# Two-layer graph network on one core: r is transposed by VectorE and DMA, W2 runs one graph later, ScalarE makes the second norm's statistics

## The reference

```
h = relu(layernorm(x))                          # per node, over 512
x = x + relu(attention(h, adj))                 # 8 heads of 64, masked softmax over neighbours
h = relu(layernorm(x))
r = relu(conv(h, adj, W1) + b1)                 # 512 -> 1024, conv mixes the nodes by adj
q = layernorm(r) * gamma + beta                 # over 1024
x = x + h + conv(q, adj, W2) + b2               # 1024 -> 512
```

## Time and profile before

| | us |
|---|---|
| median of 3 runs (2589.86 to 2593.36) | 2591.59 |
| the profiled execution | 2593.87 |
| its span, first to last instruction | 2591.9 |
| PE busy in the span | 2527.3 (98%) |
| DVE, POOL, ACT busy | 1968.6, 1630.6, 1423.3 |
| one turn in the middle | 19.52 |

### The profile page before, as it was taken

How to read it: one execution, slowest core, us unless ns; L and a number is a source line. 1 busy time by engine, 2 the same in 40 slices (tenths; PEclk the granted TensorE clock), 3 DMA queues, 4 the chain that set the end, 5 groups by cost and what they waited for, 6 DMA issues and landing times.

```text
span 2591.9 us, 50876 instructions
## 1 busy us (share of the span) xinstructions
PE 2527.3 (98%) x14996; PEld 2195.1 (85%) x14996; DVE 1968.6 (76%) x4640; ACT 1423.3 (55%) x3465; POOL 1630.6 (63%) x2068
## 2 busy tenths in 40 slices
PE   3899999999999999999999999999999999999998
PEld 2788888888888888888888888888888888888886
DVE  5877777777777777777777777777777777777774
ACT  2555555555555555555555555555555555555553
POOL 4666666666666666666666666666666666666663
PEclk8899999999999999999999999999999999999999
DMA  5122222222222222222222222222222222222210
GB/s 183 63 75 80 77 76 80 74 79 77 73 79 74 80 79 74 80 76 77 77 73 79 74 80 79 74 80 79 74 80 72 82 79 71 79 75 80 79 65 26
DMA packets 105480, 201.89 MB, mean 78 GB/s; under 512 B 20080, under 2 KB 36464, under 8 KB 105456
## 3 DMA queue, kind: packets, MB, share of 16 engines
q1 hardware_dynamic: 105456, 201.60, 23.5%
HBM read 167.39 MB, written 34.15 MB: 78 GB/s over the span
## 4 chain that ended last, share of the span: by engine, by line
PE 85%; DVE 8%; issue 3%; POOL 2%; DMA 1%; ACT 1%; SPq 0%; POOLq 0%; DVEq 0%
PE p_w1a L843 12%; PE p_w1a L839 12%; PE p_w1a L838 12%; PE p_att L917 7%; PE p_w1b L953 5%; PE p_w1b L839 5%; PE p_w1b L843 5%; PE p_w1b L838 5%; PE p_att L897 4%; PE p_fa L834 2%; PE p_fa L832 2%; PE p_fa L833 2%; PE p_fb L832 2%; PE p_fb L833 2%; PE p_fb L834 2%
## 5 line engine op out<-in xcount | busy, mean ns | idle before, releaser
L392 POOL TENSOR_TENSOR rs<-ve,halfpow 128x1 f32<-128x1 f32 x128 | 117.8, 921 | 544.8 <-DVE ve L774 544.8
L380 POOL TENSOR_TENSOR u<-u,mask 128x1024 f32<-128x1024 f32 x128 | 306.3, 2393 | 182.0 <-DMA u<-en_rows 182.0
L838 PE MATMUL p_w1a<-W_hi,rT_hi 128*128 128x512 f32 x1024 | 415.5, 406 | 0.0
L457 ACT ACTIVATE att<-u,shifts 128x128 f32<-128x128 f32 x1024 | 400.5, 391 | 18.4 <-DVE shifts L734 10.5
L839 PE MATMUL p_w1a<-W_lo,rT_hi 128*128 128x512 f32 x1024 | 404.1, 395 | 0.0
L458 ACT ACTIVATE att_low<-u,shifts 128x128 f32<-128x128 f32 x1024 | 399.5, 390 | 0.0
L843 PE MATMUL p_w1a<-W_hi,rT_lo 128*128 128x512 f32 x1024 | 280.8, 396 | 0.0
L502 ACT ACTIVATE rT_hi<-p_tb 128x512 fp32r<-128x512 f32 x128 | 76.6, 598 | 333.5 <-PE p_tb L864 333.5
L917 PE MATMUL p_att<-feats,attT 128*128 128x65 f32 x2048 | 242.9, 272 | 2.2 <-ACT attT L492 2.2
L917 PEld LDWEIGHTS p_att<-feats,attT 128*128 128x128 f32 x2048 | 239.6, 192 | 2.7 <-ACT attT L492 2.7
L789 DVE SCALAR_TENSOR_TENSOR raw<-p_w1a,rs,t_bc 128x512 f32<-128x512 f32 x128 | 96.1, 750 | 187.2 <-PE p_w1a L843 187.2
(11 more groups left out here) (125 smaller groups left out, 7216.9 us busy)
## 6 DMA issues: line engine op xcount, KB each, us to landing
u<-en_rows SPq DMA_DIRECT2D x130, 576.0 KB, 3.6
x_in<-in_x SPq DMA_DIRECT2D x128, 256.0 KB, 2.6
xT_in<-in_xT SPq DMA_DIRECT2D x128, 256.0 KB, 3.2
out<-raw SPq DMA_DIRECT2D x128, 256.0 KB, 2.0
adj_in<-in_adj SPq DMA_DIRECT2D x128, 128.0 KB, 2.5
en_rows<-eT SPq DMA_DIRECT2D x520, 1.1 KB
raw<-in_W1T SPq DMA_DIRECT2D x2, 1024.0 KB, 8.1
raw<-in_W2T SPq DMA_DIRECT2D x2, 1024.0 KB, 9.7
```

Of the source, the lines that this page charges most:

```text
L380: nc.gpsimd.tensor_tensor(u[:, g.slot(2), 0:HEADS, :], u[:, g.slot(2), 0:HEADS, :], mask[:, :].unsqueeze(1).broadcast_to([P, HEADS, N]), A ...
L392: nc.gpsimd.tensor_tensor(rs1[:, :], ve1[:, :], halfpow[:, :], ALU.pow).then_inc(s_rs1, 1)
L457: nc.scalar.activation(att[:, i, :], u[:, g.slot(2), i, :], ACT.Exp, bias=shifts[:, 0, i:i + 1])
L838: mm(dst, hi, w_hi, start=first, stop=False)
```

## The change

- **r is transposed without PE.** DVE transposes r, 128x1024, in blocks of 32x32 (STREAM_TRANSPOSE into rB); SP stores rB to a DRAM tensor r_blocks (512 KB), waits for it, and loads it back by four DMAs that put the blocks at their places (rT). Each of the four moves 1024 pieces of 32 elements (128 bytes).
- ACT rounds rT in one piece of 1024 at the end of the turn (rT_hi), DVE forms rT_lo in one piece at the start of the next turn, before the first pre. Both read rT in SBUF, where the two halves were read in PSUM.
- **W2, z and the product by G move back a graph**: in turn t PE multiplies graph t-1 by W2 and graph t-2 by G. There is one turn more at the end. The sums x + h + b2 (rest) get four places in place of two.
- **The second norm's statistics move to ACT**: the two rectifications also give row sums (accum_out), two small instructions make the mean of them, one Square of 1024 gives the sum of squares (accum_out), one small instruction the variance. DVE's bn_stats (two) and bn_aggr are gone, on POOL one of two small instructions.
- **Orders.** On ACT the first rectification goes before the rounding of the features' input, and z_hi before hg_hi. On DVE the column sum, cnt and its reciprocal go before the second pre, and the first L601 waits for rs1. The load of x is issued by ACT, that of adj by SP earlier in the turn.

The diff, cut to its core:

```diff
@@ SP
+                g = t
+                if g.within(NG):
+                    sp.wait_ge(s_rB, g.count())
+                    sp.dma_start(r_blocks[:, :], rB).then_inc(s_rB_out, 16)
+                    sp.wait_ge(s_rB_out, g.count(per=16))
+                    for c in range(4):
+                        sp.dma_start(rT[32 * c:32 * (c + 1), :].rearrange("a (k q b) -> a k q b", q=4, b=32),
+                                     r_blocks.rearrange("(q a) (k c b) -> c a k q b", q=4, c=4, b=32)[c]).then_inc(s_rT, 16)
@@ ACT
...
-                    act.wait_ge(s_rT, g.count(per=2) - 1)
...
-                    nc.scalar.activation(rT_hi[:, 0:HALF], p_ta[:, :], ACT.Copy).then_inc(s_rT_hi, 1)
+                    act.wait_ge(s_r, g.count(per=2) - 1)
...
+                    nc.scalar.activation(nm2a[:, :], sum2[:, 0:1], ACT.Copy, scale=-1.0 / DH).then_inc(s_nm2a, 1)
                     act.wait_ge(s_pre, g.count(per=2))
-                    nc.scalar.activation(r[:, HALF:DH], r[:, HALF:DH], ACT.Relu).then_inc(s_r, 1)
+                    nc.scalar.activation(r[:, HALF:DH], r[:, HALF:DH], ACT.Relu, accum_out=sum2[:, 1:2]).then_inc(s_r, 1)
...
-                    nc.scalar.activation(rT_hi[:, HALF:DH], p_tb[:, :], ACT.Copy).then_inc(s_rT_hi, 1)
+                    nc.scalar.activation(nm2[:, :], sum2[:, 1:2], ACT.Identity, bias=nm2a[:, :], scale=-1.0 / DH).then_inc(s_nm2, 1)
...
+                    nc.scalar.activation(dev, r, ACT.Square, bias=nm2[:, :], accum_out=sq2[:, :]).then_inc(s_sq2, 1)
...
+                    nc.scalar.activation(ve2[:, :], sq2[:, :], ACT.Identity, bias=eps[:, :], scale=1.0 / DH).then_inc(s_ve2, 1)
...
+                    act.wait_ge(s_rT, g.count(per=64))
...
+                    nc.scalar.activation(rT_hi[:, :], rT, ACT.Copy).then_inc(s_rT_hi, 1)
@@ DVE
+                g = t.plus(-1)
+                if g.within(NG):
+                    dve.wait_ge(s_rT_hi, g.count())
+                    nc.vector.tensor_tensor(rT_lo[:, :], rT, rT_hi[:, :], ALU.subtract).then_inc(s_rT_lo, 1)
...
-                    nc.vector.bn_stats(st2[:, 0, :], r[:, 0:HALF]).then_inc(s_stats2, 1)
...
+                    nc.vector.transpose(rB, r[:, :]).then_inc(s_rB, 1)
@@ PE
-                    pe.wait_ge(s_r, g.count(per=2) - 1)
...
-                    transposes(p_ta, r[:, 0:HALF], s_rT)
-                g = t.plus(-1)
+                g = t.plus(-2)
                 if g.within(NG):
                     pe.wait_ge(s_z_lo, g.count())
...
-                    transposes(p_tb, r[:, HALF:DH], s_rT)
...
+                g = t.plus(-1)
+                if g.within(NG):
+                    pe.wait_ge(s_rT_hi, g.count())
...
+                    for c in range(HC):
...
+                        high(p_w1a[:, :], rT_hi[:, part(c)], W2_hi[:, c, :], W2_lo[:, c, :], c == 0)
+                    pe.wait_ge(s_rT_lo, g.count())
+                    for c in range(HC):
+                        last = low(p_w1a[:, :], rT_lo[:, part(c)], W2_hi[:, c, :], c == HC - 1)
                     last.then_inc(s_w2, 1)
```

More of the change, by code:

```diff
@@ L50, in turns @@
 def turns(eng, turn, total, before={}):
-    loops = (total - AHEAD - 2) // UNROLL
-    for t in range(-AHEAD, 1):
+    loops = (total - AHEAD - 3) // UNROLL
+    for t in range(-AHEAD, 2):
         if t in before:
@@ L58, in turns @@
     with eng.Fori(0, loops) as k:
-        for u in range(1, UNROLL + 1):
+        for u in range(2, UNROLL + 2):
             turn(Graph(u, k))
-    for t in range(1 + loops * UNROLL, total + 1):
+    for t in range(2 + loops * UNROLL, total + 2):
         turn(Graph(t))
@@ L221, in _, with nth, load_x, load_adj @@
         def _(sp):
-            def load(g):
+            def nth(g):
+                return g.base if g.loop is None else g.loop * UNROLL + g.base
+            def load_x(g):
+                sp.dma_start(x_in[:, g.slot(4), :], x[bass.ds(nth(g), 1), :, :].rearrange("a p d -> p (a d)")).then_inc(s_in[g.slot(4)], 16)
+            def load_adj(g):
                 if g.has(4):
-                    sp.wait_ge(s_x1, g.count(4))
                     sp.wait_ge(s_inc, g.count(4))
@@ L229, in load @@
                     sp.wait_ge(s_row, g.count(4))
[L230 to L233, removed]
+                sp.dma_start(adj_in[:, g.slot(4), :, :], adj2[bass.ds(nth(g), 1), :, :, :].rearrange("a p t n -> p (a t) n")).then_inc(s_in[g.slot(4)], 16)
+            def load(g):
+                load_x(g)
+                load_adj(g)
             def load_xT(g):
@@ L265, in turn @@
                     load_xT(g)
+                if t.plus(5).within(NG) and (t.loop is not None or t.base >= -1):
+                    load_adj(t.plus(5))
                 if g.within(NG + 2):
@@ L273, in turn @@
                                  en_rows.rearrange("(a h) n -> a (h n)", a=1).broadcast_to([P, ROWS * N])).then_inc(s_en_bc, 16)
-                g = t.plus(-1)
+                g = t.plus(-2)
                 if g.within(NG):
                     sp.wait_ge(s_y_sb, g.count())
[L278 to L282, removed]
+                    sp.dma_start(out[bass.ds(nth(g), 1), :, :].rearrange("a p d -> p (a d)"), y[:, g.slot(2), :]).then_inc(s_out[g.slot(2)], 16)
+                g = t
[6 more added lines that the diff above has]
+                                     r_blocks.rearrange("(q a) (k c b) -> c a k q b", q=4, c=4, b=32)[c]).then_inc(s_rT, 16)
             def setup_rest():
@@ L465, in turn @@
                     exps(t.plus(1), 1)
+                g = t
+                if g.within(NG):
+                    act.wait_ge(s_pre, g.count(per=2) - 1)
+                    nc.scalar.activation(r[:, 0:HALF], r[:, 0:HALF], ACT.Relu, accum_out=sum2[:, 0:1]).then_inc(s_r, 1)
                 g = t.plus(3)
@@ L505, in turn @@
                     nc.scalar.activation(G_hi[:, :], G[:, g.slot(4), 0:N], ACT.Copy).then_inc(s_G_hi, 1)
+                g = t
+                if g.within(NG):
+                    act.wait_ge(s_sq2, g.count())
+                    if g.has(1):
+                        act.wait_ge(s_rs2, g.count(1))
+                    nc.scalar.activation(ve2[:, :], sq2[:, :], ACT.Identity, bias=eps[:, :], scale=1.0 / DH).then_inc(s_ve2, 1)
                 if t.plus(2).within(NG):
                     exps(t.plus(2), 0)
+                g = t.plus(5)
+                if g.within(NG) and (g.loop is not None or g.base >= 4):
+                    act.wait_ge(s_x1, g.count(4))
+                    n = g.base if g.loop is None else g.loop * UNROLL + g.base
+                    act.dma_start(x_in[:, g.slot(4), :], x[bass.ds(n, 1), :, :].rearrange("a p d -> p (a d)")).then_inc(s_in[g.slot(4)], 16)
                 g = t.plus(1)
@@ L520, in turn @@
                         rounded(3)
+                g = t.plus(-1)
+                if g.within(NG):
+                    act.wait_ge(s_z, g.count())
+                    if g.has(1):
+                        act.wait_ge(s_y, g.count(1))
+                    nc.scalar.activation(z_hi[:, :], z[:, :], ACT.Copy).then_inc(s_z_hi, 1)
                 g = t.plus(1)
@@ L969, in turn @@
                         pe.wait_ge(s_G_sb, g.count(1))
+                    if g.has(4):
+                        pe.wait_ge(s_y_sb, g.count(4))
                     mm(p_G, inc[:, g.slot(2), 1, :], beT[:, :], start=True, stop=True).then_inc(s_G, 1)
```

157 lines of the change are left out of this document (69 added, 88 removed).

## The result

The change takes 2605.31 us (median of six runs, 2597.54 to 2614.38) where the kernel before takes 2589.52 (2587.65 to 2593.36): a ratio of 1.0056, interval 1.0036 to 1.0077. The forecast was 2575 us. The runs spread over 17 us, those of before over 6. The profiled execution is the fastest of the six, 2597.54.

What follows compares the result with a forecast made beforehand. PE's own work was taken to bound the kernel, 128 turns of 19.52 us. Per turn -0.80 + 0.4 + 0.1 + 0.1 = -0.20, times 127 is -25, +8 at the end: -17, so 2575 us; range 2490 to 2750.

Steps and rivals of the forecast that it cites:

- What PE loses: On PE, r's eight transposes and one change of kind go: 0.36 + 0.08 + 0.36 = 0.80 us a turn.
- attT is late next: ACT's copy for PE's attention product ends at 1327.4, PE wants it at 1327.0: a wait of 0.4 us a turn.
- the unknown prices: On the way to attT: 0.1 us for the rectifications' row sums, 0.1 for rT_lo, 0 for cnt.
- rT_lo and cnt: On DVE beside POOL: rT_lo priced at 0.1 us, up to 1.5 if held; cnt at 0, up to 0.76.
- The bound for cnt: On DVE, cnt costs up to 0.76 us more if POOL's add to u comes earlier; 0 was taken.
- the 1.5 us: On DVE, the first pre's delay if rT_lo were held until POOL's xc is over.
- The DMA round trip: Block transpose 1.2, store 2.7, four gathers 6 us: lands 0.8 us before ACT wants it for rT_hi.
- the point from which it decides: Gather time, 6.7 us, from which the loop through store and gather sets the turn; this rival had 0.24.
- The ends: One turn more at the end lays the DMA round trip bare: +8 us.
- The third (contention): Rival, chance 0.18: contention and row sums cost 0.5 us more before attT, turn 19.7, total 2622 us.
- The fourth: Rival, chance 0.04: PE's wait returns elsewhere, as at L953 for ACT's h, 2560 to 2600 us.
- the first, 2498: Rival, chance 0.12: nothing is late, attT in time, all 0.80 us a turn gained, 2498 us.

Runs made afterwards that it cites:

- e6: The change with DVE's column sum behind the second pre, cnt where inv stood, reciprocal and inv behind nm1: 2552.62 us, 0.9842 of the kernel before.
- e8: The change with four extra PE transposes of the identity behind the attention product, where those of r's second half stood: 2723.82 us, 1.0521 of the kernel before.
- e7: The change with four extra PE transposes of the identity ahead of attT's wait, where those of r's first half stood: 2600.82 us, 1.0023 of the kernel before.
- e4: The change with DVE waiting for POOL's xc ahead of rT_lo, so xc is always first: 2939.2 us, 1.1308 of the kernel before.
- e5: The change itself, unaltered, measured once more on another chip: 2615.39 us, 1.0081 of the kernel before.
- e3: The change with POOL's xc waiting for rT_lo and POOL's add of the mask to u waiting for cnt: 2590.12 us, 0.9945 of the kernel before.
- e9: The change with only POOL's xc waiting for rT_lo, the add of the mask left free: 2589.48 us, 1.001 of the kernel before.
- e10: The change with only POOL's add of the mask waiting for cnt, xc left free: 2587.42 us, 0.9996 of the kernel before.
- e11: The change with SP storing the blocks twice in a row, so the gather starts 2.6 us later: 2854.59 us, 1.1041 of the kernel before.
- e1: The change with DVE's column sum, cnt and reciprocal moved back behind the second pre: 2610.15 us, 1.0021 of the kernel before.

## Why the prediction was wrong, point by point

- **What PE loses: right.** Where attT is in time (e6) PE starts the attention product at 8.72 us of the turn; forecast was 1327.0 - 1318.28 = 8.7. e8 puts the second four at 0.38 at most in a turn with rT_lo first (0.36).
- **attT is late next: right**, place and size. Its copy ends at 9.31 (1083.47 to 1092.78), forecast 9.1 and 0.2 for the unknown prices. Of those, the row sum costs 0.1 on the way each time (the read of the accumulator, from start to start), and the comparison beside POOL 0.49 in place of 0.28. Turn 19.35, forecast 19.32. e7 shows the other side of it: of the 0.80 taken off PE, the 0.44 ahead of the wait are worth nothing.
- **That the kernel before waits for nothing else: not so.** The prediction took a turn as PE's own work, from a view with five waits. Two turns of that kernel, of 19.43 and 19.88 us, with ACT's h and PE's first product from it:

```profile
568.87 0.81 ACT L517 ACTIVATE h<-x,nb,rs 128x512 f32<-128x512 f32 x1 [1.52 <-POOL nb L346]
569.98 1.05 PE L953 MATMUL p_w1b<-G,h 128*128 128x128 f32 x8
```

```profile
667.61 0.81 ACT L517 ACTIVATE h<-x,nb,rs 128x512 f32<-128x512 f32 x1 [2.10 <-POOL nb L346]
668.47 1.16 PE L953 MATMUL p_w1b<-G,h 128*128 128x128 f32 x8 [0.18 <-ACT h L517]
```

From the starts of the turns (552.69 and 650.80) h ends at 16.99 and at 17.62, and PE begins its product at 17.29 and, 0.05 behind h, at 17.67. Over the loop no turn is under 19.4 us, and above that its length follows the end of h; the mean is 19.58, not the 19.52 of the one turn that was read. These waits are mostly under 0.15 us after the modelled end of the product before, so the view leaves them out, and the busy share of 98% hides them. So h was already late by 0.16 us a turn on average, and of the 0.80 only as much could be had as h comes earlier too: e6, with attT in time, reaches 19.14.
- **rT_lo and cnt: this step failed.** The prediction said "I take 0.1, since rT_lo is there first, by 0.5" and of cnt "I take 0". Both values hold in a usual turn. But they were margins of 0.5 and 0.7 us between engines whose times vary by as much from turn to turn, and I priced them by one turn. I also left out what POOL does right before xc, in the turn that was read across the 1319.88 at which rT_lo was to start:

```profile
1319.15 1.31 POOL L425 TENSOR_TENSOR z_lo<-raw,z_hi 128x512 fp32r<-128x512 f32 x1
```

So xc starts when z_lo ends, and that moves with the length of the turn before (e4, e8). In every fourth turn DVE is 0.35 later and the first margin is 0 to 0.25; when it is lost, the second one (1.1 us less) is gone as well, or nearly. The bound for cnt, 0.76 by its longest row, was low too, because none of those rows was held from the start of a 2.4 us add: 2.24 is. That PE's clock would fall in the wait was in no term. In the profiled execution the five slow turns cost 9.1 us and the late cnt of the second turn up to 5.3, together 14 of the 20.7 that it lies above the forecast. Over all runs the change (2605.31, and 2615.39 in e5) lies 15 to 28 us above e3, e9 and e10 (2590.12, 2589.48, 2587.42), on other chips. The ratios give no firmer size: 0.9945, 1.001 and 0.9996 against 1.0056 and 1.0081.
- **With the races settled the forecast still isn't met.** e3's profiled execution took 2588.89 where 2577 was forecast. Its three first turns cost 1.8 more than before, its tail 2.6 more than forecast, and its turns are 0.14 shorter than those before, not 0.20: 8 us. That last part is about the price of the wait of xc (19.44 against 19.36 in the change's turns without the slow ones). So the races are the largest part of what was off, but not all of it.
- **The Trainium skill**, SBUF — State Buffer, section Who interferes with whom, has the rule for it (whoever issues first holds the shared ports to the end), and the trace agrees in both directions: xc 2.29 for 1.31, rT_lo 2.37 for 1.2. rT_lo at 1.62 behind z_lo is the same rule. The section also counts tensor_scalar, which is what cnt is, among the instructions that can take both ports. The trace agrees: cnt took 2.24 us for 0.17. I used the rule to rule out the 1.5 us, but it says that the order of issue decides, and that varies here.
- **The DMA round trip: right, by luck with the margin.** The first gather is issued 2.6 us behind the store, the four issues take 3.7 us, and rT_hi starts without a wait 6.45 us after the first. The forecast was 6, and 6.7 as the point from which it decides; with the gather 2.6 us later ACT waits for it (e11), so there is such a point, but e11 doesn't say how close. The pieces took more than the 9.7 ns of the estimate. Of the queue from 1095.9 to 1101.9 us (packets, MB, share of 16 engines):

```profile
q1 hardware_dynamic: 4237, 0.68, 66.9%
```

That is 0.669 x 16 x 6.0 / 4237 = 15 ns each, some larger ones among them. The estimate worked out from the Trainium skill, VectorE: DVE Perf Modes, section The three transpose paths, was 8.2 us, 2.0 of it landing time from rows 10. The trace, with at most 6.45, doesn't bear that out for pieces of 128 bytes.
- **The ends: too low.** The tail costs 11.8, not 8, and the start with the first three turns 9.6 more, which I had left out, 5.3 of it the second turn with its late cnt.
- In the profiled execution these add up: 9.6 (start and first three turns), 3.8 (tail), 9.1 (slow turns), -1.2 (usual turns) make 21.3, where 20.7 lie between forecast (2577) and measurement (2597.54). That the other runs take up to 17 us more fits with more slow turns in them (no such spread with the races settled), but they have no trace.
- **Rivals.** The third (contention) had the mechanism and, with 2622, the side, but as a constant delay in each turn. Its sum is off: 0.5 more than taken on a turn of 19.32 makes 19.8 and not 19.7, so about 2638. The fourth was right that h is next: it takes what attT leaves (e1, e6), as it already took some in the kernel before, so the first, 2498, could not have come about by an attT in time alone.

## What to carry to other kernels

Where two engines can hold each other off, look at the smallest margin over all turns, not at that of one, and ask what the loser queues: if the next race hangs on the first, the cost is a cascade. A wait that fixes the order is cheap but not free (the wait of xc cost 0.08 us a turn, the one of the add nothing that shows), and moving the short instructions off the late path into idle time (e6, 63 us below the change on the same chip) was worth more than the change itself saved (0.21 us in each usual turn, 27 us). Before an edit is credited with time on the bounding engine, ask on which side of its next wait that time stands. And where an engine seems always busy, compare the lengths of many turns with the end of the results it takes: if the length follows one of them, the engine is waiting.

## What was not expected of the hardware

- A two-column instruction on DVE (cnt, 0.17 us) took 2.24 us beside a POOL instruction of 2.37 us that had started 0.16 earlier.
- Behind a wait of 1.3 us PE's granted clock was 0.50 for some 3 us in a turn of 21.8 (e5); behind the same wait in a turn of 20.2 it stayed at 1.00, so that the same held rT_lo costs 0.9 or 2.4 us.
- 0.4 us more work on PE made the turns 0.85 us longer on average (e8, +108 us), by shifting who comes first between two other engines.
